# Relative values of an attention layer: table stationary in column strips, probabilities streaming, and new places for the pieces of work

## The chip, the cores and the metric

The kernel is one program on one core of a Trainium2 chip. The metric is the device time of one launch in microseconds (us), median of several executions. All data are fp32. The engines are PE (TensorE: weight loads and matmuls), DVE (VectorE), ACT (ScalarE), POOL (GpSimd), and SP (SyncE), which here only issues transfers.

## The reference, cut to what matters

A batch of 8 sequences of 256 tokens with 128 features passes two layers, each an attention and a feed-forward part with a residual. The change touches only the first attention: 16 heads of 8 features, with learned relative keys and relative values, clipped at a distance of 20.

```python
pos = jnp.arange(S)                                   # S = 256
idx = jnp.clip(pos[None, :] - pos[:, None], -MAX_REL, MAX_REL) + MAX_REL   # MAX_REL = 20
rk2 = rel_k[idx]; rv2 = rel_v[idx]
attn1 = jnp.einsum('bhqd,bhkd->bhqk', q, k)
attn2 = jnp.einsum('bhqd,qkd->bhqk', q, rk2)          # relative scores
attn = jax.nn.softmax((attn1 + attn2) / scale, axis=-1)
w1 = jnp.einsum('bhqk,bhkd->bhqd', attn, v)
w2 = jnp.einsum('bhqk,qkd->bhqd', attn, rv2)          # relative values
x = (w1 + w2).transpose(0, 2, 1, 3).reshape(B, S, E)
out = x @ Wo.T + bo
```

After it come (all unchanged): an attention over the heads of one token with a gated mixture of 8 matrices ("feed"), a Taylor attention ("second"), and a mixture of experts with routing ("late").

## The kernel before

One sequence is called a batch t here, from 0 to 7. Its work is cut into pieces: `norm0` to `blocks` (layer norm, projections, tables of queries), `scores`, `turn`, `relative`, `keep_rv`, `weigh`, `back`, `divide`, `project_out` (first attention), `norm1` to `experts` (feed), `norm3` to `turn4` (second), `route` to `store` (late). Every engine has its own list of pieces of all batches. The list is made from a table of numbers, one for each piece and engine (`ENGINE_AT`, with corrections in `MOVED` for batches 0, 6 and 7): batch t's piece stands at t * 480 plus its number, and the engine works through the pieces in that order and no other. So pieces of three or four batches alternate on each engine. Between engines there are only semaphores.

The first attention of a batch, in the words that the rows use:

- A row group i holds 8 queries of all 16 heads: 128 rows. There are 32 groups, 16 in each half c of the queries. `scores` takes two groups of each half (a quad; 8 quads): L1147 multiplies block-diagonal queries `qbd` with the keys `kT` (256 columns), L1157 adds the relative scores from `qr` and a table `tkw`. Both work in four 64x64 quarters of PE's array at once. DVE takes row maxima (`nmx`, L832), ACT the exponentials (`pm`, L547).
- `turn` transposes `pm` (L1168); ACT moves the result to `pT` (L555).
- `relative` (L1186, and L1189 for the groups near the border of the halves): for each group i the 128x128 probabilities `pT` are the stationary operand and a stretch of the table `tv` is the moving one. Its 64 useful columns are 8 possible distances x 8 features; each of the 128 rows needs the 8 of its own query, and the rest is computed for nothing. The number of columns is 128 for 24 of the 32 groups and 64 for 8. There are 16 such pieces in a batch, one after about each `turn`. ACT copies the sums to `rvs` four times a batch (`keep_rv`, L531).
- SP then stores, for each of the 8 queries of a group, the wanted 8 columns to DRAM (L457, 8 transfers) and, when all have landed, loads them back as `relo` (L460, L462), rows being queries now (`relative_out`).
- `weigh` (L1210) multiplies the probabilities with the values: `v9` is stationary in four column strips of 32, `pT` streams with 128 columns. `back` (L1221) transposes the sums, and `divide` on DVE adds `relo` (L840) and divides by the sums of the probabilities. Then come `turn_out`, `project_out` and the feed part, whose longest DVE stretch begins with `prod<-q,kv` (L883).

SP's queue, in its order: for batch t first `relative_out(t - 1)`, then the load of `xin` for t + 1, then `rows(t + 1)`: queries to DRAM (L439) and back in another layout, `qc` (L448), from which POOL makes `qr`.

Of the kernel before, what the change touches and what calls it, by code (L numbers as in the profile page):

```python
# [100 lines left out]
FEED_AT = [585, 592, 602, 611, 626, 643, 652, 662, 664, 670, 673, 673, 673, 684, 699, 704, 707, 713, 718, 740, 741, 743,  # L101
           759, 774, 781, 813, 816, 840, 855, 882, 907, 910, 920, 946, 958, 963]
# [3 lines left out]
SECOND_AT = [974, 1031, 1059, 1088, 1112, 1141, 1156, 1173, 1175, 1177, 1192, 1220, 1221, 1227, 1236, 1257, 1268, 1274,  # L106
             1303, 1358]
LATE = once("route", "rank") + counted("chunk", NCH + 2) + once("turn_rw") + counted("join", 1 + NP) + once("store")
LATE_AT = [1360, 1366, 1378, 1392, 1408, 1427, 1436, 1442, 1475, 1527, 1555, 1579, 1597, 1630, 1638, 1657, 1659, 1660,
           1675, 1701, 1733, 1760, 1800, 1812]  # L110
LISTS = ("PREPARE", "ATTENTION", "FEED", "SECOND", "LATE")
ALL = PREPARE + ATTENTION + FEED + SECOND + LATE
ALL_AT = PREPARE_AT + ATTENTION_AT + FEED_AT + SECOND_AT + LATE_AT
ENGINE_AT = {"PE": [-445.5, -339, -278, -249.5, -90, 113, 163, 0, 60, 120, 177.5, 241, 302.5, 360, 420, 38.5, 77, 96, 144.5,
# [15 lines left out]
             "DVE": [-354.5, -314, -290.5, -188, -88, 87, 141, 0, 60, 120, 178.5, 240, 301.5, 357.5, 420, 43, 65, 90, 131.5, 143,  # L130
# [1360 lines left out]
```

## Time and profile before

| what | value |
|---|---|
| time, median of 3 runs | 733.3 us (732.82 to 733.8) |
| span of the profiled execution, first to last instruction | 736.6 us |
| PE busy, matmuls | 646.7 us (88%) |
| DVE busy | 548.8 us (75%) |
| ACT busy | 381.3 us (52%) |
| POOL busy | 146.1 us (20%) |
| mean granted TensorE clock, share of full | 0.958 |

The page does not give the profiled execution's own device time beside its span; the span alone is 3.3 us (0.45%) above the median. The busy time of an engine is the union of its instructions' times, and a matmul's end is modelled, so that neighbours on PE overlap a little. What a row of matmuls costs PE is therefore read better from the start of one row to the start of the next than from its duration. An fp32 matmul stands in the trace as two records with a weight load each.

### The profile page before, as it was taken

To read this page: it belongs to the slowest core of one execution; us is meant where nothing else is said; L and a number is where in the kernel's file an instruction comes from. 1 tells how busy PE (TensorE), PEld (TensorE's weight loads), DVE (VectorE), ACT (ScalarE), POOL (GpSimd) and SP (SyncE) were. 2 spreads that over 40 slices of the span, in tenths; PEclk is the share of its full clock that TensorE was granted. 3 is DMA by queue.
4 is the path that set the end of the run, shared out by engine and by line. 5 is a ranking of instruction groups with operands and counts; after the bars stand their busy time and mean duration, and the time that the engine had idled before them with its cause. 6 is when DMAs were issued, how large, how long until landed. Compare 5 with 4: busy or idle time off the path is not lost.

```text
span 736.6 us, 16761 instructions
## 1 busy us (share of the span) xinstructions
PE 646.7 (88%) x6432; PEld 517.3 (70%) x6432; DVE 548.8 (75%) x1337; ACT 381.3 (52%) x907; POOL 146.1 (20%) x178
## 2 busy tenths in 40 slices
PE   2698577987999999999999999899999998789987
PEld 1576355765787688778876788678876886467666
DVE  2432596679868986899689976898779966977375
ACT  3375245456655654674566565575466454413532
POOL 2413201330233023300521051302330012010100
PEclk9799589999999999999999999999999999887999
DMA  5502000200110002000210011000200010000000
GB/s 132 227 2 24 14 1 9 23 9 1 15 16 10 1 16 22 11 1 1 27 21 1 1 24 16 9 1 9 30 2 1 2 15 9 1 8 0 2 8 7
DMA packets 75908, 13.43 MB, mean 18 GB/s; under 512 B 69803, under 2 KB 74933, under 8 KB 75701
## 3 DMA queue, kind: packets, MB, share of 16 engines
q1 hardware_dynamic: 73202, 10.78, 8.1%
q8 instruction: 51, 0.84, 0.5%
q0 software_dynamic: 384, 1.05, 0.5%
q10 hardware_dynamic: 2244, 0.55, 0.3%
q14 instruction: 27, 0.22, 0.1%
HBM read 8.95 MB, written 3.16 MB: 16 GB/s over the span
## 4 chain that ended last, share of the span: by engine, by line
PE 41%; DVE 28%; issue 18%; ACT 6%; POOL 3%; DMA 2%; SPq 1%; POOLq 0%; ACTq 0%; DVEq 0%
PE bank L1147 5%; DVE prod L883 5%; DVE lg L889 4%; PE bank L1168 4%; PE bank L1354 4%; PE bank L1270 4%; PE bank L1355 3%; DVE prod L908 3%; PE bank L1210 3%; DVE at L914 3%; DVE nmx L832 3%; ACT pm L547 3%; PE bank L1186 3%; PE bank L1157 2%; DVE xo L1062 1%
## 5 line engine op out<-in xcount | busy, mean ns | idle before, releaser
L547 ACT ACTIVATE pm<-bank,nmx 128x256 f32<-128x256 f32 x256 | 100.3, 480 | 58.7 <-DVE nmx L832 58.5
L832 DVE TENSOR_REDUCE nmx<-bank 128x2 f32<-128x512 f32 x128 | 82.1, 683 | 44.5 <-PE bank L1157 44.4
L555 ACT ACTIVATE pT<-bank 128x512 f32<-128x512 f32 x128 | 76.5, 598 | 65.0 <-PE bank L1168 64.0
L1147 PE MATMUL bank<-kT,qbd 64*64 64x256 f32 x1024 | 87.7, 405 | 10.4 <-POOL qr L657 9.3
L1168 PE MATMUL bank<-w,pm 128*128 128x128 f32 x512 | 81.9, 284 | 16.2 <-ACT pT L555 10.0
L612 ACT ACTIVATE ha<-bank,w 128x256 f32<-128x256 f32 x104 | 49.6, 477 | 67.5 <-PE bank L1355 67.5
L1168 PEld LDWEIGHTS bank<-w,pm 128*128 128x128 f32 x512 | 59.8, 145 | 29.8 <-ACT pm L547 15.9
L1186 PE MATMUL bank<-tv,pT 128*128 128x128 f32 (+1 forms) x512 | 79.7, 278 | 0.2 <-ACT pT L555 0.2
L1042 DVE SCALAR_TENSOR_TENSOR hu<-bank,w,ha 128x256 f32<-128x256 f32 x104 | 49.9, 480 | 36.5 <-ACT ha L612 35.7
L1186 PEld LDWEIGHTS bank<-tv,pT 128*128 128x128 f32 x512 | 70.0, 195 | 6.0 <-issue 4.4
L1354 PE MATMUL bank<-xfT,w 128*128 128x256 f32 x208 | 67.7, 408 | 3.7 <-DVE hu L1042 3.5
L1355 PE MATMUL bank<-xfT,w 128*128 128x256 f32 x208 | 63.3, 387 | 0.0
L706 POOL TENSOR_TENSOR rs_c<-ve_c,expo 128x2 f32<-128x2 f32 x8 | 5.6, 699 | 273.8 <-DVE ve_c L788 273.8
L1157 PE MATMUL bank<-tkw,qr 64*64 64x96 f32 (+1 forms) x1024 | 55.5, 265 | 0.0
L1157 PEld LDWEIGHTS bank<-tkw,qr 64*64 64x64 f32 x1024 | 46.5, 139 | 12.2 <-issue 1.2
L961 DVE SCALAR_TENSOR_TENSOR x<-bank,gl,x 128x128 f32<-128x128 f32 x128 | 35.9, 344 | 23.3 <-PE bank L1270 23.2
L597 ACT ACTIVATE sq<-bank,half_root 128x512 f32<-128x512 f32 x64 | 40.4, 684 | 18.8 <-PE bank L1309 18.6
L1147 PEld LDWEIGHTS bank<-kT,qbd 64*64 64x64 f32 x1024 | 32.3, 138 | 24.9 <-issue 20.8
L1381 PE MATMUL bank<-w,hu 128*128 128x256 f32 x128 | 41.3, 405 | 4.5 <-DVE xo L1062 3.6
L1355 PEld LDWEIGHTS bank<-xfT,w 128*128 128x128 f32 x208 | 40.5, 195 | 5.6
L657 POOL TENSOR_TENSOR qr<-qc,half_mask 128x512 f32<-128x512 f32 x31 | 33.4, 1097 | 54.1 <-DMA qc<-d_qdh 54.1
L1354 PEld LDWEIGHTS bank<-xfT,w 128*128 128x128 f32 x208 | 33.7, 194 | 14.4 <-DVE hu L1042 9.7
(203 smaller groups left out, 1294.1 us busy)
## 6 DMA issues: line engine op xcount, KB each, us to landing
w<-wpack_dram SPq DMA_DIRECT2D x1, 3944.0 KB, 11.9
xin<-x_in_dram SPq DMA_DIRECT2D x8, 128.0 KB, 2.1
d_qdh<-qdh SPq DMA_DIRECT2D x8, 128.0 KB, 1.8
d_rv<-rvs SPq DMA_DIRECT2D x64, 16.0 KB, 2.2
out_dram<-xo POOLq DMA_DIRECT2D x8, 128.0 KB, 2.3
qc<-d_qdh SPq DMA_DIRECT2D x15, 64.0 KB, 3.7
tv<-d_ev SPq DMA_DIRECT2D x1, 736.0 KB, 4.5
w<-wpack_dram SPq DMA_DIRECT2D x1, 513.0 KB, 5.2
```

Source lines behind the costliest of these rows:

```text
L547: a = act.activation(pm[:, s % 2, c, j], b_s[c][:, j * S:(j + 1) * S], exp, bias=nmx[:, i:i + 1])
L555: act.activation(view(pT, (c * RTC + 2 * s) * C * P, [[1, 2 * C * P]]), b_t[:], copy).then_inc(pT_ready[0], 1)
L612: act.activation(ha[:, n % 2], late_bank(t, "chunk", n)[:, 0:S], idn, scale=0.5, bias=wc("b1", IN_TURN[n], IN_TURN[n] + 1)).then_inc(a_rea ...
L832: v.tensor_reduce(nmx[:, i:i + 2], b_s[c][:].rearrange("p (j k) -> p j k", j=2), AX_X, ALU.max, negate=True).then_inc(max_ready[0], 1)
L1042: v.scalar_tensor_tensor(hu[:, n], late_bank(t, "chunk", n)[:, S:2 * S], wc("b3", IN_TURN[n], IN_TURN[n] + 1), ha[:, n % 2], ALU.add, ALU. ...
L1147: mm(b_s[c][cols:cols + P // 2, j * S:(j + 1) * S], qbd[rows:rows + P // 2, i], kT[rows:rows + P // 2, t % 2, u], start=True, stop=False, ...
L1157: a = mm(b_s[c][cols:cols + P // 2, j * S + lo:j * S + hi], qr[rows:rows + P // 2, i], tkw[rows:rows + P // 2, KB // QI - 1 - i % (KB // Q ...
L1168: a = nc.tensor.transpose(b_t[:, (j * 2 + kc) * P:(j * 2 + kc + 1) * P], chunk(pm[:, s % 2, c, j], kc), ident)
L1186: a = mm(b_rv[:, at:at + n], pT[:, i, c], tv[:, v0 * D0:v0 * D0 + n], start=True, stop=not corner)
L1354: mm(bk[:, 0:S], wc("W1", q * P, q * P + P), xfT[:], start=True, stop=True)
L1355: mm(bk[:, S:2 * S], wc("W3", q * P, q * P + P), xfT[:], start=True, stop=True).then_inc(ab_ps[0], 1)
L1381: mm(o, chunk(hu[:, 3 * n + 2], c), wc("W2rem", e * E, (e + 2) * E), start=True, stop=False, skip_group_check=True)
```

## The change

`relative` becomes two pieces in a batch instead of 16, each for half of the row groups of both halves c. The operands change places: four table rows (four distances x 8 features, 32 columns) are the stationary operand in one of PE's four column strips, and the probabilities of four queries of all heads (64 columns) stream. A piece has 32 such matmuls and 5 more near the borders (74 in a batch against 38 before). ACT copies the sums twice in a batch instead of four times and sorts them on the way (a read with a step of four elements). SP stores four times for each copy, once for each quarter that a query needs, and loads four times; the first half of this goes between the load of `xin` and `rows(t + 1)`, the second after `rows(t + 1)`. `relo` now has features in the outer place, and `divide` reads it with a step. Half of `Wo`'s rows change places for one of the two halves (`wo_turned`, loaded once), and `weigh` counts its heads in another order. The relative scores take only the columns in which the table is not zero: 27 to 83 (46, 46, 46, 51, 59, 67, 75, 83 within each 64 queries, less where the sequence ends) instead of 96 or 128. All numbers of places are new, with corrections for every batch on every engine.

```diff
+QG = P // D0 // 4            # 4 queries
+RG = P // QG
-            def relative_values(t, x):
-                s, c = divmod(x, C)
-                pe.wait_ge(*raised(pT_ready, t, x + 1))
-                ...
-                for j in range(2):
-                    i = c * RTC + 2 * s + j
-                    at = (c * 4 + i % 4) * QI * D0
-                    n = QI * D0 * (2 if i % 4 < 3 else 1)
-                    v0 = S - QI - i % RTC * QI - TV0
-                    corner = RTC - CORNER <= i < RTC + CORNER
-                    a = mm(b_rv[:, at:at + n], pT[:, i, c], tv[:, v0 * D0:v0 * D0 + n], start=True, stop=not corner)
-                    if corner:
-                        ...
+            def relative_values(t, n):
+                pe.wait_ge(*raised(pT_ready, t, HALVES // 2 * (n + 1)))
+                pe.wait_ge(*raised(rv_kept, t, n))
+                ...
+                for T in range(4 * n, 4 * n + 4):
+                    for c in range(C):
+                        for j in range(4):
+                            g = 4 * T + j
+                            out_ = b_rv[j * MT:(j + 1) * MT, (c * 4 + T % 4) * QG * H0:(c * 4 + T % 4 + 1) * QG * H0]
+                            cols = lambda kc: view(pT, ((c * RTC + g // 2) * C + kc) * P + g % 2 * QG, [[QI, H0], [1, QG]])
+                            window = lambda table, x: table[:, x * D0:x * D0 + MT]
+                            a = mm(out_, window(tv, S - QG - QG * g - TV0), cols(c), start=T % 4 == 0 and c == 0, stop=True,
+                                   skip_group_check=True, tile_position=(0, j * MT))
+                            ends = g >= (P - REL) // QG if c == 0 else g < REL // QG
+                            if ends:
+                                ...
+                                a = mm(out_, window((tv_right, tv_left)[c], x), cols(1 - c), start=False, stop=True,
+                                       skip_group_check=True, tile_position=(0, j * MT))
+                a.then_inc(rv_ps[0], 1)
@@ scores, relative part
-                        at = u * KB - NEAR
-                        lo, hi = max(0, at), min(S, at + WIN)
+                        at, first = u * KB - NEAR, i * QI
+                        lo, hi = max(0, min(u * KB, first - REL + 1)), min(S, first + QI + REL - 1)
@@ keep_rv on ACT
-                    act.activation(view(rvs, n * S, [[RTC * QI * D0, C], [1, S]]), b_rv[:], copy).then_inc(rv_kept[0], 1)
+                    act.activation(view(rvs, n * 512, [[QG * H0, 512 // (QG * H0)], [H0, QG], [1, H0]]),
+                                   view(b_rv, 0, [[QG * H0, 512 // (QG * H0)], [1, QG], [QG, H0]]), copy).then_inc(rv_kept[0], 1)
@@ SP
+            def relative_out(t, n):
+                sp.wait_ge(*raised(rv_kept, t, n + 1))
+                ...
+                for q in range(QG):
+                    ...
+                    sp.dma_start(dst, src).then_inc(rv_out[0], 16)
+                sp.wait_ge(*raised(rv_out, t, 16 * QG * (n + 1)))
+                row = C * E
+                for q in range(QG):
+                    dst = bass.AP(relo[:].tensor, (n * P // 2 + q) * row, [[QG * row, RG // 2], [E, C], [1, E]])
+                    sp.dma_start(dst, d_rv[q, n].rearrange("c g d h -> g c (d h)")).then_inc(relo_in[0], 16)
             for t in range(B):
-                if t:
-                    relative_out(t - 1)
                 if t < B - 1:
                     ...  # xin for t + 1
+                relative_out(t, 0)
+                if t < B - 1:
                     rows(t + 1)
-            relative_out(B - 1)
+                relative_out(t, 1)
@@ divide on DVE
-                                    view(relo, n * E, [[D0, H0], [1, D0]]), ALU.add).then_inc(o_steps[0], 1)
+                                    view(relo, n * E, [[1, H0], [H0, D0]]), ALU.add).then_inc(o_steps[0], 1)
@@ tables at the start, DVE: tv comes in as rows and is copied once with a step
+                v.tensor_copy(view(tv, 0, [[MT, TV // QG], [QG, D0], [1, QG]]),
+                              view(hu, 0, [[MT, TV // QG], [1, D0], [D0, QG]])).then_inc(tables_ready[0], 1)
```

PE's order where a batch in the middle of the program goes from its last row groups to `weigh` (L1210 before): before, the last relative matmuls stand in three places between transpositions, expert matmuls (L1354, L1355) and the feed's products (L1270).

```order
L1168 MATMUL bank<-w,pm 128x128 x4
L1186 MATMUL bank<-tv,pT 128x128
L1189 MATMUL bank<-tv_right,pT 128x128
L1186 MATMUL bank<-tv,pT 128x64
L1189 MATMUL bank<-tv_right,pT 128x64
L1270 MATMUL bank<-w,hT 128x256 x2
L1186 MATMUL bank<-tv,pT 128x128
L1186 MATMUL bank<-tv,pT 128x64
L1354 MATMUL bank<-xfT,w 128x256
L1355 MATMUL bank<-xfT,w 128x256
L1210 MATMUL bank<-pT,v 32x128 x32
```

In the changed kernel (line numbers are its own: L1401 is `weigh`, L1375 and L1380 `relative`, L1461 the feed's products, L1545 and L1546 the expert matmuls) the same place reads:

```order
L1401 MATMUL bank<-pT,v 32x128 x32
L1461 MATMUL bank<-w,hT 128x256 x2
L1545 MATMUL bank<-xfT,w 128x256
L1546 MATMUL bank<-xfT,w 128x256
L1358 MATMUL bank<-w,pm 128x128 x4
L1461 MATMUL bank<-w,hT 128x256 x2
L1545 MATMUL bank<-xfT,w 128x256
L1546 MATMUL bank<-xfT,w 128x256
L1375 MATMUL bank<-pT,tv 32x64 x20
L1380 MATMUL bank<-pT,tv_right 32x64
L1375 MATMUL bank<-pT,tv 32x64 x5
L1380 MATMUL bank<-pT,tv_right 32x64
```

The first `weigh` now stands ahead of the last `turn` and of the second `relative` block, which is one lump of 37 matmuls.

SP's queue before, one batch of it with what each transfer waits for:

```order
L439 DMA d_qdh<-qdh 128x2x128 [waits qc_in,qdh_ready]
L448 DMA qc<-d_qdh 64x32x8 [waits qr_ready,qdh_out]
L448 DMA qc<-d_qdh 64x32x8
L457 DMA d_rv<-rvs 16x32x8 [waits on_ready,rv_kept]
L457 DMA d_rv<-rvs 16x32x8 x7
L460 DMA relo<-d_rv 128x128 [waits rv_out]
L462 DMA relo<-d_rv 128x64 x2
L473 DMA xin<-x_in_dram 128x2x128 [waits xres_ready,xn_ready]
```

And in the changed kernel (L639 stores, L644 loads of `relo`, L620 and L629 `rows`, L656 `xin`):

```order
L656 DMA xin<-x_in_dram 128x2x128 [waits xres_ready,xn_ready]
L639 DMA d_rv<-rvs 32x8x16 [waits on_ready,rv_kept]
L639 DMA d_rv<-rvs 32x8x16 x3
L644 DMA relo<-d_rv 16x2x128 [waits rv_out]
L644 DMA relo<-d_rv 16x2x128 x3
L620 DMA d_qdh<-qdh 128x2x128 [waits qc_in,qdh_ready]
L629 DMA qc<-d_qdh 64x32x8 [waits qr_ready,qdh_out]
L629 DMA qc<-d_qdh 64x32x8
L639 DMA d_rv<-rvs 32x8x16 [waits rv_kept]
L639 DMA d_rv<-rvs 32x8x16 x3
L644 DMA relo<-d_rv 16x2x128 [waits rv_out]
L644 DMA relo<-d_rv 16x2x128 x3
```

The first half of the stores and loads now stands ahead of the next batch's `rows`, the second half behind it.

## Rows read from the trace of the kernel before

**Rows 1.** The page, part 1: busy us (share of the span) and instructions.
```profile
PE 646.7 (88%) x6432; PEld 517.3 (70%) x6432; DVE 548.8 (75%) x1337; ACT 381.3 (52%) x907; POOL 146.1 (20%) x178
```

**Rows 2.** Windows: stretch, length, busy us (instructions) by engine, clock, DMA share, GB/s.
```profile
20.80:62.40 41.60, 35.33 (x410) 28.41 (x410) 13.81 (x27) 25.41 (x61) 9.98 (x12) 0.90 0.28 97
62.40:135.30 72.90, 52.46 (x589) 41.84 (x591) 45.23 (x88) 31.03 (x76) 15.66 (x18) 0.81 0.08 10
135.30:205.20 69.90, 60.45 (x707) 47.59 (x710) 55.84 (x133) 39.81 (x96) 17.50 (x22) 1.00 0.09 11
...
285.20:365.20 80.00, 76.94 (x809) 62.52 (x812) 67.10 (x164) 46.62 (x113) 18.53 (x22) 1.00 0.08 11
...
524.60:603.00 78.40, 74.44 (x791) 60.74 (x790) 65.35 (x154) 44.46 (x104) 10.56 (x14) 1.00 0.04 7
603.00:736.60 133.60, 112.47 (x717) 85.38 (x716) 92.63 (x258) 47.36 (x106) 12.28 (x15) 0.92 0.03 6
```

**Rows 3.** Chain of waits in order of time: start us, us, what.
```profile
94.15 2.36 DVE prod L883 x2
...
159.41 2.36 DVE prod L883 x2
...
626.46 2.36 DVE prod L883 x2
```

**Rows 4.** PE's timeline, relative matmuls of batch 4: start us, us, what.
```profile
318.25 0.83 PE L1186 MATMUL bank<-tv,pT 128*128 128x128 f32 x6
318.93 0.39 PE L1189 MATMUL bank<-tv_left,pT 128*128 128x128 f32 x2
319.15 0.33 PE L1186 MATMUL bank<-tv,pT 128*128 128x64 f32 x2
319.32 0.39 PE L1078 MATMUL bank<-w,xn 128*128 128x128 f32 x2
```

**Rows 5.** PE's timeline: a `weigh` piece and a quad of scores.
```profile
285.17 1.95 PE L1210 MATMUL bank<-pT,v 128*32 128x128 f32 x64
287.06 1.13 PE L1270 MATMUL bank<-w,hT 128*128 128x256 f32 x4
...
288.98 0.66 PE L1147 MATMUL bank<-kT,qbd 64*64 64x256 f32 x8
289.46 0.40 PE L1157 MATMUL bank<-tkw,qr 64*64 64x96 f32 x8
289.63 0.67 PE L1147 MATMUL bank<-kT,qbd 64*64 64x256 f32 x8
...
290.44 0.70 PE L1354 MATMUL bank<-xfT,w 128*128 128x256 f32 x2
```

**Rows 6.** PE's timeline: two matmuls with eight columns.
```profile
352.91 0.51 PE L1348 MATMUL bank<-w,xfT 128*128 128x8 f32 x4
353.27 0.64 PE L1186 MATMUL bank<-tv,pT 128*128 128x128 f32 x4
```

**Rows 7.** SP's timeline, stores and loads of relative values, batch 3, then batch 0.
```profile
284.98 6.08 SPq L457 DMA_DIRECT2D d_rv<-rvs  x8
...
292.98 0.91 SPq L462 DMA_DIRECT2D relo<-d_rv  x2
```

**Rows 8.** DVE's timeline, the addition that uses them in `divide`.
```profile
75.21 0.29 DVE L840 TENSOR_TENSOR on<-bank,relo 128x128 f32<-128x128 f32 x1 [3.95 <-DMA relo<-d_rv]
...
296.49 0.23 DVE L840 TENSOR_TENSOR on<-bank,relo 128x128 f32<-128x128 f32 x1
```

**Rows 9.** Waits: who for whom, us in total, times, longest.
```profile
PE bank L1221 <- DVE on L840: 5.2, 3, 4.4
```

**Rows 10.** Groups by line on ACT: busy us, mean ns | idle before, releaser.
```profile
L531 ACT ACTIVATE rvs<-bank 128x512 f32<-128x512 f32 x32 | 19.2, 600 | 7.1 <-PE bank L1186 7.1
```

**Rows 11.** The page, part 6: transfers, KB each, median us to landing.
```profile
d_rv<-rvs SPq DMA_DIRECT2D x64, 16.0 KB, 2.2
relo<-d_rv SPq DMA_DIRECT2D x16, 32.0 KB, 2.0
```

More of the change, by code:

```diff
@@ L146 @@
-MOVED = {0: [-488, -493, -365, -195, -212, -252, -189, 0, 0, 0, 0, 0, 0, 0, 0, 9, -11, 5, 12, 10, 10.5, 10, 6, -1, 7, 5,
[18 rows of a table removed]
-PIECES = sorted([(at, k, piece) for k, (piece, at) in enumerate(zip(ALL, ALL_AT))])
-def in_turn(at):
-    placed = [(t * PERIOD + at[k] + (MOVED[t][k] if t in MOVED else 0), k, t) for k in range(len(ALL)) for t in range(B)]
+ENGINE_AT = {
[8 rows of a table added]
+    "ACT": [-392.5, -327, -654, -451, -75.5, 57, 229, 0, 60, 157.9, 164, 245, 301.5, 360, 420, 46.3, 59.8, 106, 164.1, 165, 199.7, 217,
[6 rows of a table added]
+    "DVE": [-354.5, -807, -290.5, -188, -300, 87, 141, 0, 92.8, 120, 178.5, 240, 346.8, 357.5, 420, 43, 65, 90, 131.5, 143, 166, 203,
[6 rows of a table added]
+    "POOL": [-321.6, -292, -217.5, -205, -147.5, -27, 38, 0, 60, 120, 178.5, 245, 301.5, 360, 420, 12, 64, 91, 168.5, 181, 193, 215,
[6 rows of a table added]
@@ new lines, with in_turn @@
+MOVED = {
[61 rows of a table added]
+    "ACT": {0: {0: -488, 1: -493, 4: -212, 5: -252, 6: -189, 7: 46.2, 10: 35.8, 16: -11.3, 18: -6.3, 19: 10, 22: 6, 23: 14.5, 28: 15, 29:
[56 rows of a table added]
+    "DVE": {0: {0: -488, 2: -365, 3: -195, 5: -252, 6: -189, 9: 23.1, 15: 9, 16: -11, 17: 5, 18: 12, 19: 10, 20: 10.5, 21: 10, 22: 6, 23:
[54 rows of a table added]
+    "POOL": {0: {0: -481.9, 1: -493, 2: -365, 3: -195, 4: -212, 5: -252, 6: -98.9, 15: 9, 16: -11, 17: 5, 18: 12, 19: 10, 20: 10.5, 21: 10,
[33 rows of a table added]
+def in_turn(engine):
+    at, moved = ENGINE_AT[engine], MOVED[engine]
+    placed = [(t * PERIOD + at[k] + moved.get(t, {}).get(k, 0), k, t) for k in range(len(ALL)) for t in range(B)]
@@ L170, in in_turn @@
     return [(t, ALL[k]) for _, k, t in sorted(placed)]
-TURNS = {engine: in_turn(at) for engine, at in ENGINE_AT.items()}
-assert len(ALL_AT) == len(ALL)
+TURNS = {engine: in_turn(engine) for engine in ENGINE_AT}
+assert all(len(at) == len(ALL) for at in ENGINE_AT.values())
 W_COLS = [("ident", P), ("head_mask", H0), ("query_mask", QI), ("head_mask3", H1), ("earlier", NE * NE), ("half", P),
@@ L267, in build @@
         pT = sb("pT", P, RT, C, P)
-        rvs = sb("rvs", P, RT, QI * D0)
-        relo = sb("relo", P, C, E)
+        rvs = sb("rvs", P, 2, 512)
+        relo = sb("relo", P, C, D0, H0)
+        wo_turned = sb("wo_turned", P, E)
         oT = sb("oT", P, C, 512)
@@ L325, in build @@
         ek, ev = sq[:].rearrange("p h c q -> p (h c q)")[:, 0:EK], hu[:].rearrange("p n s -> p (n s)")[:, 0:EV * D0]
+        tv_rows = hu[:].rearrange("p n s -> p (n s)")[:, 0:TV * D0]
         ht = sb("ht", P, 2, S)
@@ L448, in rows @@
                     sp.dma_start(*own_rows(half)).then_inc(qc_in[0], 16)
[L450 to L462 removed]
+            def relative_out(t, n):
+                sp.wait_ge(*raised(rv_kept, t, n + 1))
+                if n == 0:
+                    sp.wait_ge(*raised(on_ready, t, 0))
+                for q in range(QG):
+                    src = bass.AP(rvs[:].tensor, (QG - 1 - q) * 2 * 512 + n * 512 + q * H0, [[QG * 2 * 512, P // QG], [QG * H0, 512 // (QG * H0)], [1, H0]])
+                    dst = bass.AP(d_rv.tensor, (q * 2 + n) * C * E * RG // 2, [[H0, P // QG], [H0 * P // QG, 512 // (QG * H0)], [1, H0]])
+                    sp.dma_start(dst, src).then_inc(rv_out[0], 16)
[4 more added lines that the diff above has]
+                    sp.dma_start(dst, d_rv[q, n].rearrange("c g d h -> g c (d h)")).then_inc(relo_in[0], 16)
             rows(0)
@@ L466, in _ @@
             sp.dma_start(w[:, n0:], wpack[:, n0:]).then_inc(w_in1[0], 16)
+            for half in range(2):
+                to = (1 - half) * P // 2
+                sp.dma_start(wo_turned[to:to + P // 2], wc("WoT", p0=half * P // 2, p1=(half + 1) * P // 2)).then_inc(turned_in[0], 16)
             for t in range(B):
-                if t:
-                    relative_out(t - 1)
                 if t < B - 1:
@@ L1121, in piece @@
                     pe.wait_ge(*raised(onT_ready, t, 1))
+                    if t == 0:
+                        pe.wait_ge(turned_in[0], 32)
                     for c in range(C):
-                        a = mm(chunk(b_o, c), chunk(onT, c), wc("WoT"), start=True, stop=True)
+                        a = mm(chunk(b_o, c), chunk(onT, c), wo_turned[:] if c else wc("WoT"), start=True, stop=True)
                     a.then_inc(wo_ps[0], 1)
@@ L1206, in weigh @@
                             h = i * PER + j
-                            v0 = (kc + C * (kc != c)) * V9 + h * (D0 + 1)
-                            row = (h + c * D0) % H0 * QI
+                            v0 = (kc + C * (kc != c)) * V9 + (h + c * D0) % H0 * (D0 + 1)
+                            row = h * QI
                             a = mm(b_o[j * MT:(j + 1) * MT, i * P:(i + 1) * P], v9[:, v0:v0 + MT],
```

60 lines of the change are left out of this document (14 added, 46 removed), and 276 rows, old and new, of tables (ENGINE_AT, MOVED).

## The prediction

> **What bounds the kernel now.** I read the page's busy times first, then windows cut at the start of each batch's `weigh`, then PE's timeline inside one window. PE leads with 646.7 of 736.6 us, DVE follows with 548.8 [rows 1]. The windows show where that holds. From 205.2 to 603.0 us five batches pass at (603.0 - 205.2) / 5 = 79.6 us each, and in the one that stands there PE is busy 76.9 of 80.0 us, DVE 67.1, ACT 46.6, at the full clock [rows 2]. So PE's own work sets the period, with some 3 us of waits; DVE would allow 13 us less. The head is another matter. Batch 0's attention takes 41.6 us with PE busy for 35.3, and the next 72.9 us hold 52.5 us of PE work at a granted share of 0.81, part of it at the lower level of 1.2 GHz [rows 2]: there PE waits for DVE's feed stretch, which begins at 94.15 us for batch 0 and at 159.41 for batch 1 [rows 3]. From the feed stretch of batch 7 at 626.46 to the end are 110 us that hold no first attention any more [rows 3].
>
> **Relative values, before.** Starts give the price: from 318.25 to 319.32 us there are ten records, five matmuls, so 0.214 us each [rows 4]. A batch has 38: 8.1 us.
>
> **Relative values, after.** The old trace has no 64-column stream in strips; the nearest row is `weigh`, the same array form and the same operand streaming with 128 columns: 32 matmuls from 285.17 to 287.06, 0.236 us for each four that run side by side [rows 5]. That is about what one full-array matmul of 128 columns costs (0.214), so the four share the time and the columns set it. That loading can set it instead is seen at eight columns: 0.18 us a matmul for 128 weight columns [rows 6]; 32 columns would need a quarter, 0.045 (estimate). With 64 columns a four should cost 0.118; if nothing came from the shorter stream, 0.236. A block has 37 matmuls, 9.25 fours: 1.1 to 2.2 us. Two extras. Ten border matmuls a batch follow another in the same strip; if each waits for its predecessor they add at most 10 x 0.107 (half the 128-column price) = 1.1 us. And changing the form of the array costs something: in a quad the first pair of groups takes 0.65 us (288.98 to 289.63), the second, which ends in a change to the full array, 0.81 [rows 5]; two blocks have four such changes, up to 0.64 us. Ends for a batch: 2.2 and 6.1 us. I take 3.5, near the lower end because `weigh` shows columns, not loads, as the price. Saved: 4.6 us a batch.
>
> **Relative scores.** Four matmuls of 256 columns and four of 96 and 128 take the 0.65 us above, so columns set that too: 384 columns, 1.7 ns each. The widest of a four falls from 128 to 46, 46, 46, 51, 59, 67, 75 and 83, 59 on average: 0.117 us less for each of 16 fours, 1.9 us a batch; nothing if the next weights can't come sooner. I take 1.6, because loading 64 columns (half of 0.18 us) would still hide. The Trainium skill, TensorEngine Tiling (Array Packing), section "Instruction Overhead", says that a matmul of one column lasts as long as one of about 60. By that rule five of the eight widths count as 60, the mean is 66, and the saving 1.7 us instead of 1.9; no run here shows it yet.
>
> **What this does to the period.** PE's work falls by 6.2 us (2.0 to 7.9). What is late next is the answer of the stores. Before, the first store goes out at 284.98, the last load at 292.98 to 293.89, and DVE adds at 296.49: 11.5 us [rows 7, 8]. Now half of it has gone earlier; the rest is a copy (0.6) [rows 10], four stores at 6.08 / 8 = 0.76, four loads at 0.91 / 2 = 0.46, and two landings, 2.2 and 2.0 [rows 7, 11]: 9.7 us. In the new order two quads (2.9), `weigh` (1.9), a transposition (0.4) and six pairs of full-array matmuls (about 0.96 each, from 287.06 to 288.98 for two [rows 5]) stand between the second block and the first `back`: 11 us. It just covers; behind `back`, `divide` on DVE and everything behind it in DVE's order would wait, and PE's second `back` with it. Such waits were 5.2 us in all before [rows 9]. I charge 0.8 us a batch for this and for DVE being 90% full. Period: 79.6 - 5.4 = 74.2 us, bounds -1.2 to -7.9 (the gain of 2.0 less the 0.8, and 7.9 with no new wait). Five periods: -27 us (-6 to -40).
>
> ACT loses two copies a batch, 1.2 us, behind PE. Its reads now step by four elements; were they twice as slow, the two would cost what the four did. That sits in the chain to `divide` alone, 0.6 us. The one more copy of `tv` at the start and the load of `wo_turned` lie beside DMA and PE work of the head, long before their users; if not, 2 us once. In SP's queue `rows(t + 1)` now waits for the first half's stores, some 3.0 + 2.2 us and a copy; `relative 0` stands far ahead of the last row groups, and a batch's `rows` had some 15 us before its scores, so I charge nothing.
>
> **Head and tail.** Batch 0's attention loses 8.1 us of PE work that stood between its quads and gets 3.5 back in two lumps: -4. Its `divide` had waited 3.95 us for `relo` on DVE, and PE 4.4 us with it [rows 8, 9]: -4. Then batch 1's scores now fill PE while DVE does batch 0's feed stretch, so batch 1's attention is over when that stretch ends, and PE spends less of these 72.9 us at the low clock: of the 65.3 us between the two feed stretches [rows 3] I take 5 off. Together -13 (-4 to -20). The interval to batch 2 is bound less by PE (60.5 of 69.9 us): -2. The tail has the same work in nearly the same order: 0 (3 either way).
>
> Sum against the profiled span: 736.6 - 27 - 13 - 2 = 694.6 us. The median lies 3.3 us under that span, so 691.5, say **692 us**.
>
> **Rivals.** (a) Less: waits take the place of the matmuls. In favour: DVE goes from 84 to 90% full and the cover of the store chain is about 1 us. Against: PE waits only 3 us a period now. With -2 a period, -8 in the head and -1: 736.6 - 19 - 3.3 = 714. (b) More: the new places also take out half of PE's present waits, and the head gives its full 20: -7.9 x 5 - 20 - 3 is 62, 671; a middle case 677. DVE's 67 us a period leave room for it. (c) The strips don't run side by side at 64 columns: 74 x 0.107 + 0.64 = 8.6 us, nothing saved, and only the scores' 1.6 a batch stay, less the waits: about -1 a period and -7 in the head, 721. Against it stands `weigh`, whose strips do. (d) Slower: the two blocks are bound by how fast PE can begin instructions. A batch has 148 records there instead of 76; from (8.1 - 0.64) / 148 = 50 ns a record the relative values save nothing, and from 61 ns the scores' 1.6 us are gone too. At 70 ns a period is 1.3 us longer, and the lump ahead of `weigh` costs the head as much: 733.3 + 6 x 1.3 is 741. Against it: `weigh` has 64 records in 1.89 us, 30 ns each, while it streams [rows 5]. A rule of the Trainium skill lies in this direction: TensorE: Matmul & The Clock Gate, section "Wait — 56ns, not 53.3ns?", gives about 62 ns a matmul where the sequencer's program decodes it and 25 ns as the floor otherwise. By the first figure relative values would cost 9.8 us a batch and the kernel would be slower as in (d); the 30 ns of `weigh` say that it doesn't hold in this run.
>
> **How the numbers follow.** The forecast, in a band of some 9 us either way, 0.56; (a) 0.20; (b) 0.13; (c) 0.05; (d) 0.04; a change of nothing 0.02. The range from 674 to 717 holds the forecast, nearly all of (a) and most of (b), and leaves out (c), (d) and the far ends. The likeliest case alone is 683 to 702. What a measurement can tell from no change is about 0.2%, 1.5 us. Faster 0.94, the same 0.02, slower 0.04.
>
> **What would show it.** In the profile after: the starts of `weigh` in the middle 73.5 to 75.5 us apart; 32 + 5 matmuls of a relative block in 1.3 to 2.2 us from its start to the next row's; a quad in 1.2 to 1.3 us instead of 1.46; DVE 88 to 92% busy in a period and PE near 95%, at the full clock; batch 1's feed stretch at 142 to 152 us. Wrong would be: a block over 3 us, records in it more than 50 ns apart, the clock under 0.95 in the middle, or DVE's wait for `relo` in every batch.

## The result, and the profile after

The changed kernel takes 729.7 us (median of 20 runs, 723.5 to 736.3), beside 736.0 us for the kernel before (20 runs on the same chips). The ratio is 0.9916, with a 95% interval of 0.9889 to 0.9943: 0.8% faster, some 6 us, where 41 were predicted and the range ended at 717. The profiled execution has a span of 729.2 us (before 736.6).

The page of the changed kernel, part 1, answers to [rows 1]:

```profile
PE 605.6 (83%) x7008; PEld 462.2 (63%) x7008; DVE 565.3 (78%) x1338; ACT 374.3 (51%) x891; POOL 148.5 (20%) x178
```

PE has lost 41.1 us of busy time; 8 x 6.2, some 50, were forecast. DVE, from which nothing was taken, is 16.5 us busier. Both lines matter below. The windows of the changed kernel, cut at the starts of `weigh` as in [rows 2]:

```profile
21.00:70.20 49.20, 33.14 (x510) 23.84 (x514) 16.12 (x30) 24.39 (x58) 16.07 (x16) 0.78 0.26 85
70.20:121.50 51.30, 36.90 (x550) 26.66 (x538) 38.44 (x70) 27.38 (x65) 6.78 (x8) 0.83 0.09 14
121.50:192.80 71.30, 56.57 (x769) 40.77 (x768) 57.78 (x125) 37.25 (x93) 14.98 (x18) 0.91 0.05 8
274.90:350.30 75.40, 69.28 (x873) 54.19 (x872) 68.06 (x156) 45.95 (x111) 18.29 (x21) 1.00 0.06 10
510.70:593.30 82.60, 75.45 (x961) 58.16 (x960) 71.26 (x177) 47.72 (x112) 15.48 (x18) 1.00 0.06 8
593.30:729.20 135.90, 109.85 (x709) 83.94 (x708) 93.62 (x254) 45.86 (x104) 13.14 (x16) 0.92 0.02 6
```

Read by this mark, the five middle periods last (593.3 - 192.8) / 5 = 80.1 us, against 79.6 before, and the whole gain seems to lie in the head. The mark misleads: in the new order `weigh` of a batch stands elsewhere against the feed stretch of the batch before. DVE's feed stretch keeps its place in the batch, so its first instruction is the better mark. DVE's timeline of the changed kernel at these four places, for batches 0, 1, 2 and 7 [rows 3]:

```profile
99.04 2.36 DVE L1071 TENSOR_TENSOR prod<-q,kv 128x1024 f32<-128x1024 f32 x2
...
158.70 2.36 DVE L1071 TENSOR_TENSOR prod<-q,kv 128x1024 f32<-128x1024 f32 x2
...
230.08 1.22 DVE L1071 TENSOR_TENSOR prod<-q,kv 128x1024 f32<-128x1024 f32 x1
...
618.12 1.23 DVE L1071 TENSOR_TENSOR prod<-q,kv 128x1024 f32<-128x1024 f32 x1
```

Before, these stood at 94.15, 159.41, 233.19 and 626.46. So batch 0 is 4.9 us later, batch 1 is 0.7 earlier, the interval from 1 to 2 gives 2.4 more, the five intervals from 2 to 7 give 5.2, and the tail takes 0.9 back: -0.7 - 2.4 - 5.2 + 0.9 = -7.4, the difference of the two spans. From here on "the five intervals" means this stretch between the feed of batch 2 and that of batch 7. Its window (length, PE busy, PEld, DVE, ACT, POOL, granted clock, DMA share, GB/s), in the kernel before:

```profile
233.19:626.46 393.27, 375.16 (x3890) 304.53 (x3882) 329.25 (x798) 225.40 (x540) 78.20 (x92) 1.00 0.07 10
```

and in the changed kernel:

```profile
230.08:618.12 388.04, 350.96 (x4227) 272.49 (x4226) 339.23 (x797) 220.57 (x528) 79.57 (x92) 0.98 0.07 11
```

PE's busy time falls by 24.2 us, but its idle time (length less busy) rises from 18.1 to 37.1 us. That is the riddle of this case in two lines: PE's work was taken away, and PE waits instead. For what, the waits of the changed kernel in this stretch tell (who for whom, us in total, times, longest):

```profile
PE bank L1266 <- DVE hh L1121: 5.6, 3, 3.2
PE bank L1475 <- ACT k L773: 3.8, 5, 0.8
PE bank L1266 <- DVE hh L980: 3.2, 2, 2.7
PE bank L1412 <- DVE on L1028: 3.1, 4, 1.3
PE bank L1432 <- DVE q L1060: 3.1, 3, 1.7
```

Many waits of 0.8 to 3.2 us, on DVE and ACT, of many kinds and few of each. The longest is the first. PE's, DVE's and POOL's timeline of the changed kernel around it:

```profile
423.05 3.27 DVE L1121 TENSOR_SCALAR hh<-xl,rs_b 128x128 f32<-128x128 f32 x2
423.45 0.73 POOL L878 TENSOR_TENSOR x<-x,xl 128x256 f32<-128x256 f32 x1
424.14 2.08 POOL L837 TENSOR_TENSOR qbd<-qT,half_mask 128x512 f32<-128x512 f32 x2
...
426.37 0.47 PE L1266 MATMUL bank<-w,hh 128*128 128x128 f32 x1 [3.22 <-DVE hh L1121]
```

`scale2`, two DVE instructions that take 0.28 us each elsewhere, lasts 3.27 us here. The second of the two alone takes 2.82, the longest of its kind, and ends at 426.32, just behind POOL's sum `x2` and two `qbd` products (423.45 to 426.22). PE stands for 3.22 us, and then runs at a lower clock. Three windows of the changed kernel, before the gap, behind it and later:

```profile
418.00:423.00 5.00, 4.93 (x60) 3.90 (x58) 4.89 (x18) 3.74 (x12) 1.70 (x3) 1.00 0.11 17
426.30:432.90 6.60, 6.53 (x79) 5.83 (x80) 5.20 (x20) 1.89 (x5) 3.76 (x4) 0.59 0.29 19
434.00:440.00 6.00, 5.98 (x97) 4.88 (x96) 3.63 (x12) 2.62 (x5) 1.34 (x2) 1.00 0.01 3
```

The mean granted clock is 0.59 for 6.6 us, most of it at the lower level of 1.2 GHz, between two stretches at the full 2.4. The prediction had priced neither.

The parts that it did price are there. PE's timeline of the changed kernel, `weigh`, a block of relative values (43 of its 74 records stand in the row shown), and a quad [rows 4, 5]:

```profile
274.91 1.95 PE L1401 MATMUL bank<-pT,v 128*32 128x128 f32 x64
...
280.07 0.81 PE L1375 MATMUL bank<-pT,tv 128*32 128x64 f32 x43
...
281.32 0.70 PE L1545 MATMUL bank<-xfT,w 128*128 128x256 f32 x2
...
298.36 0.66 PE L1337 MATMUL bank<-kT,qbd 64*64 64x256 f32 x8
298.85 0.29 PE L1347 MATMUL bank<-tkw,qr 64*64 64x59 f32 x8
...
299.62 0.70 PE L1471 MATMUL bank<-h3T,w 128*128 128x256 f32 x2
```

A block takes 281.32 - 280.07 = 1.25 us, a quad 299.62 - 298.36 = 1.26.

### The profile page after: what moved, and what is told of

Its sections match the earlier page's. It is cut to its first block, busy times and chain, and to the rows that moved or that the text cites. A ratio compares the mean times of both kernels' runs of the same rounds, so it can differ in the third digit from the quotient of the medians.

```text
span 729.2 us, 17909 instructions
## 1 busy us (share of the span) xinstructions
PE 605.6 (83%) x7008; PEld 462.2 (63%) x7008; DVE 565.3 (78%) x1338; ACT 374.3 (51%) x891; POOL 148.5 (20%) x178
## 4 chain that ended last, share of the span: by engine, by line
issue 36%; PE 29%; DVE 16%; DMA 6%; POOL 6%; ACT 4%; SPq 3%; POOLq 0%; ACTq 0%; DVEq 0%
PE bank L1545 3%; PE bank L1337 3%; PE bank L1461 3%; PE bank L1546 3%; PE bank L1358 3%; DVE nmx L1020 2%; PE bank L1500 2%; DVE at L1102 2%; DVE xo L1250 2%; DVE hh L1121 1%; DVE prod L1096 1%; PE bank L1401 1%; PE bank L1266 1%; DMA xin<-x_in_dram 1%; DMA d_rv<-rvs 1%
## 5 line engine op out<-in xcount | busy, mean ns | idle before, releaser
L733 ACT ACTIVATE pm<-bank,nmx 128x256 f32<-128x256 f32 x256 | 100.4, 483 | 34.5 <-DVE nmx L1020 34.1
L1358 PE MATMUL bank<-w,pm 128*128 128x128 f32 x512 | 86.7, 295 | 20.7 <-ACT pT L741 12.4
L1337 PE MATMUL bank<-kT,qbd 64*64 64x256 f32 x1024 | 85.5, 425 | 15.3 <-POOL qr L843 11.0
L1358 PEld LDWEIGHTS bank<-w,pm 128*128 128x128 f32 x512 | 61.7, 150 | 38.3 <-issue 19.1
L1545 PE MATMUL bank<-xfT,w 128*128 128x256 f32 x208 | 69.3, 416 | 5.1 <-DVE hu L1230 5.1
L1546 PE MATMUL bank<-xfT,w 128*128 128x256 f32 x208 | 64.2, 391 | 0.0
L1347 PEld LDWEIGHTS bank<-tkw,qr 64*64 64x64 f32 x1024 | 42.2, 145 | 19.7 <-issue 5.1
L1337 PEld LDWEIGHTS bank<-kT,qbd 64*64 64x64 f32 x1024 | 28.9, 143 | 31.0 <-issue 20.2
L1546 PEld LDWEIGHTS bank<-xfT,w 128*128 128x128 f32 x208 | 41.2, 198 | 6.1
L1545 PEld LDWEIGHTS bank<-xfT,w 128*128 128x128 f32 x208 | 33.8, 197 | 14.9 <-DVE hu L1230 10.3
L1500 PE MATMUL bank<-q3h,k 64*128 64x256 f32 x256 | 36.5, 402 | 7.8 <-ACT sq L783 5.7
L1572 PE MATMUL bank<-w,hu 128*128 128x256 f32 x128 | 39.5, 391 | 2.8 <-DVE xo L1250 1.4
L1574 PEld LDWEIGHTS bank<-w,hu 128*128 128x128 f32 x256 | 38.5, 190 | 3.4
L837 POOL TENSOR_TENSOR qbd<-qT,half_mask 128x512 f32<-128x512 f32 x32 | 34.0, 1084 | 29.7 <-issue 20.0
## 6 DMA issues: line engine op xcount, KB each, us to landing
hu<-d_ev SPq DMA_DIRECT2D x1, 736.0 KB, 4.6
```

What stands on the lines that cost most here:

```text
L733: a = act.activation(pm[:, s % 2, c, j], b_s[c][:, j * S:(j + 1) * S], exp, bias=nmx[:, i:i + 1])
L1337: mm(b_s[c][cols:cols + P // 2, j * S:(j + 1) * S], qbd[rows:rows + P // 2, i], kT[rows:rows + P // 2, t % 2, u], start=True, stop=False, ...
L1347: a = mm(b_s[c][cols:cols + P // 2, j * S + lo:j * S + hi], qr[rows:rows + P // 2, i], tkw[rows:rows + P // 2, KB // QI - 1 - i % (KB // Q ...
L1358: a = nc.tensor.transpose(b_t[:, (j * 2 + kc) * P:(j * 2 + kc + 1) * P], chunk(pm[:, s % 2, c, j], kc), ident)
L1500: a = mm(taylor_bank(t, 2 * n + half)[:, kc * S:(kc + 1) * S], chunk(k3[rows:rows + P // 2], kc), q3h[rows:rows + P // 2, n], start=True, ...
L1545: mm(bk[:, 0:S], wc("W1", q * P, q * P + P), xfT[:], start=True, stop=True)
```

## The experiments

Times are medians; each ratio is to runs of the kernel before on the same chip, with its 95% interval. Theory C: in the new order POOL and DVE collide, and the feed stretch, with all that waits for it, is late. Theory D: DVE's own work in that stretch sets the period. Theory O: the new places cost what the arithmetic gave. Two more, W and P, were formed from the first results; the other letters (N, S, P', F, G) are told where they come up.

**One wait more on POOL.**

```
  elif name == "turn2":
      pool.wait_ge(*raised(y_ready, t, 1))
      pool.wait_ge(*raised(x3_ready, t - 1, 0))
+     pool.wait_ge(*raised(h2_ready, t, 1))
```

> The changed kernel with one wait more: POOL begins the sum x2 (and the qbd products queued behind it) only when DVE has finished scale2 (hh<-xl), so that the two no longer run at once. Theory C (collisions of POOL and DVE in the new order stretch the feed stretch's critical operations): hh<-xl falls from a mean of 905 ns to 350-460, the gap ahead of turn2 on PE goes, and the time falls by 6 to 14 us from 729.7, to 716-724. Theory D (DVE's feed stretch, with its own work, sets the period): DVE loses some 9 us in all by it, of which a part shows, 724-729. Theory O (the new places are at fault): no change within 3 us.

Measured: 718.2 us, ratio 0.9740 (0.9699 to 0.9782), 1.8% better than the changed kernel's 0.9916, by a wait. The group of `scale2` in the changed kernel, and then in this one, whose lines stand one further down (busy us, mean ns | idle before):

```profile
L1121 DVE TENSOR_SCALAR hh<-xl,rs_b 128x128 f32<-128x128 f32 x16 | 13.9, 905 | 1.9 <-POOL rs_b L874 1.7
```

```profile
L1122 DVE TENSOR_SCALAR hh<-xl,rs_b 128x128 f32<-128x128 f32 x16 | 5.5, 393 | 1.9 <-POOL rs_b L874 1.7
```

The five intervals of this kernel:

```profile
227.16:605.83 378.67, 345.35 (x4227) 267.67 (x4226) 333.88 (x797) 220.44 (x528) 79.80 (x92) 1.00 0.07 11
```

The same 4227 PE instructions take 5.6 us less, with the clock at 1.00 in place of 0.98, and PE's idle time falls from 37.1 to 33.3. In the whole launch PE waits 2.7 us for `scale2` instead of 9.2. Theory C holds, and its price lies inside what it expected: a collision of two engines and a PE gap behind it. How much of the clock's part belongs to it, the next section asks.

**The same wait in the kernel before.**

> The kernel before with the same one wait (POOL's sum x2 and the blocks behind it begin after scale2). A control: if the collision is one of the new order, it brings little here, where hh<-xl has a mean of 462 ns against 905: -1 to -4 us, ratio to before 0.995 to 0.999. If the wait is simply good for any order of this kernel, -8 to -12 us, ratio 0.984 to 0.989, and the change itself would then be worth as little as it seemed.

Measured: 742.0 us, 1.0053 (1.0018 to 1.0087). Not even the small gain: `scale2` falls from 462 to 279 ns here as well, and the kernel is 0.5% slower, which no theory had. POOL's sum `x2` now stands 17.2 us in all for `scale2`, against 3.7 in the changed kernel with the wait; that this is the 0.5% isn't shown. So the wait is no general good, and the gain above belongs to the order that the change brought.

**A second wait, for `xn`.** On top of the first:

```
  elif name == "qkv3":
      ...
      pool.wait_ge(*raised(o3_back, t, 0))
+     if t + 3 < B:
+         pool.wait_ge(*raised(xn_ready, t + 3, 1))
```

> The kernel with the wait for scale2, and a second one: POOL begins the q3h products only when DVE has finished xn of the batch three further on. In the profile of the first wait alone, xn is stretched by 6.4 us in 9 of 16 instances, each while POOL runs q3h or the sum xl. Theory C: xn falls to 350-450 ns, 3 to 5 us of DVE time go, and as turn0 and the projections of the next batch wait for it, 1 to 5 us of the time: 713-717. Theory N (xn is early enough that nobody waits): 718, the same within 2 us, or 1 to 3 us slower if q3h is late for the second attention.

Measured: 712.9 us, 0.9658 (0.9609 to 0.9707). `xn` falls from a mean of 736 ns to 340. The five intervals:

```profile
223.61:599.77 376.16, 344.86 (x4227) 268.19 (x4226) 331.55 (x797) 220.50 (x529) 83.81 (x94) 1.00 0.07 11
```

The time lies where theory C had it; theory N, by which nobody waits for `xn`, had 718. With both waits the kernel is 3.4% faster than the kernel before, and PE's busy time in the five intervals is 30.3 us under that of before, close to the prediction's 5 x 6.2 = 31, at the full clock.

**POOL's products in halves.** Each `qbd` and `qr` instruction of the kernel with both waits becomes two:

```
- g.tensor_tensor(view(qbd, i * P // 2, [[P // 2, QI], ...
+ for m in range(0, QI, QI // 2):
+     a = g.tensor_tensor(view(qbd, (i + m) * P // 2, [[P // 2, QI // 2], ...
```

> The kernel with both waits, and POOL's products qbd and qr cut into two instructions of half the size each. With the waits, hb, bi, sc and hh still last 0.9 to 1.1 us instead of 0.17 to 0.34 where one of these products (1.07 us) runs. Theory C (a colliding DVE instruction has to wait until the POOL instruction under way is over): those instances come down to 0.55 to 0.65 us, and the time falls by 1 to 4 us from 712.9, to 709-712. Theory S (POOL takes a share of DVE's rate as long as it is busy): the instances last as long as before, and the time stays or rises by 1 to 2 us, since two halves cost POOL more than one whole.

Measured: 711.2 us, 0.9622 (0.9575 to 0.9670). The intervals overlap, so a gain in time isn't shown. The mechanism is. Here are POOL's and DVE's timelines of the kernel with whole products, and then with halves, where `hb` meets them:

```profile
284.07 2.55 POOL L843 TENSOR_TENSOR qr<-qc,half_mask 128x512 f32<-128x512 f32 x2
...
284.59 2.12 DVE L983 TENSOR_SCALAR hb<-x,mv_c,rs_c 128x128 f32<-128x128 f32 x2
```

```profile
283.97 1.66 POOL L838 TENSOR_TENSOR qbd<-qT,half_mask 128x256 f32<-128x256 f32 x2
285.59 2.02 POOL L846 TENSOR_TENSOR qr<-qc,half_mask 128x256 f32<-128x256 f32 x3
...
285.06 1.23 DVE L987 TENSOR_SCALAR hb<-x,mv_c,rs_c 128x128 f32<-128x128 f32 x2
```

Two `hb` instructions last 2.12 us beside whole products and 1.23 beside halves; alone they take 0.34 each. Here DVE's instruction waits until the POOL instruction under way is over; theory S, by which POOL takes a share of DVE's rate, would have left them as long. The Trainium skill, SBUF — State Buffer, section "Who interferes with whom", says this of DVE's modes that use two ports, which `tensor_scalar` can enter: whichever engine issues first has the shared pair for the whole instruction, and the other is blocked. The traces agree, by 2.12 against 1.23 us. The prediction had not weighed it. One POOL instruction is the usual price but not the most: the `scale2` instruction of 2.82 us above was held across three that followed one another. What decides that, no run shows.

**The new arithmetic at the old places.** The old tables for all engines; the two blocks at the places of relative pieces 7 and 15:

```
+ KEPT = list(range(31)) + [38, 46, 48, 50] + list(range(51, ...))
+ placed = [(t * PERIOD + at[o] + ..., k, t) for k, o in enumerate(KEPT) ...]
```

> The changed arithmetic (strips, trimmed scores, stores that pick) at the places of the kernel before; the two blocks stand where the eighth and the sixteenth relative piece stood, all engines' tables are the old ones. Theory O (the new places are at fault): the saved 5 to 6 us of PE work a batch now show in the period, 74-76 us, and the time is 692-708. Theory D (DVE's feed stretch sets the period whatever PE saves): the middle period stays at 79-80 us, and the head's gain, which came from the order, is lost: 728-740. Theory C: between the two, 715-728, since the collisions go back to those of before.

Measured: 747.8 us, 1.0156 (1.0119 to 1.0193): 1.6% slower than before. Its five intervals:

```profile
235.66:634.16 398.50, 350.31 (x4254) 268.11 (x4246) 333.65 (x798) 220.59 (x530) 78.15 (x92) 0.99 0.07 10
```

PE is busy for 24.9 us less than before and idle for 48.2 instead of 18.1. Theory O falls, and more than that: the places are what made the change a gain, 1.0156 - 0.9916 = 2.4%, 18 us. And the saved PE work by itself made nothing faster. The waits, in the same stretch of this kernel:

```profile
PE bank L1315 <- ACT sq L598: 7.3, 5, 1.8
PE bank L1081 <- DVE hh L795: 6.0, 5, 1.5
PE bank L1173 <- ACT pT L556: 5.1, 9, 1.7
PE bank L1387 <- DVE xo L1065: 4.8, 5, 2.5
```

In the kernel before the same pieces stood for 1.5 us (`sq`), 3.3 (`hh`), 1.3 (`pT`) and 2.5 (`xo`) in its five intervals. PE reaches each of its waiting pieces earlier, and the answer of ACT or DVE isn't there.

**The old arithmetic at the new places**, eight pieces in each lump, ACT's copies moved up so that they can follow:

```
+ PLACE = list(range(31)) + [31] * 8 + [32] * 8 + [33] * 2 + [34] * 2 + ...
```

> The arithmetic of before (16 relative pieces with the values streaming, four copies, wide scores) at the new places: eight pieces at the place of each block, on ACT the copies moved up so that they can follow. Theory O: the new order costs the middle what the arithmetic gave, so this kernel is slower than before by 15 to 30 us, 750-765. Theory D: PE's work of 76.9 us a period is under what the order gives it anyway, the head gains as it did: 728-740. A price of its own: the stores leave only behind the second block, so divide may wait for relo by 2 to 4 us a batch, up to 25 us in all.

Measured: 823.1 us, 1.1187 (1.1140 to 1.1235), far outside all that was expected. PE alone waits 12.5 us for the copies that a lump of eight pieces needs in its midst, and DVE waits up to 7.0 us at a time for ACT's `ha` (4.3 before). It shows that the new places fit the new arithmetic only; for what the order is worth by itself it is no clean measure.

**DVE's work cut, in the changed kernel and in the one with both waits.**

```
- view(q1, ..., [[D0, H0 // 2], [0, H0], [1, D0]]),
+ view(q1, ..., [[D0, H0 // 2], [0, H0], [1, D0 // 2]]),
```

> The changed kernel with DVE's dot products of the feed stretch over 8 of the 16 dimensions of a head (the other half is left out): 8 operations of 1.2 us become 0.6 to 0.65, so DVE's stretch is 4.5 to 5 us shorter a batch, with PE's work as it is. Theory D: nearly all of it shows where that stretch bounds, 3.5 to 5 us in each of seven intervals, 25 to 35 us: 695-705. Theory O: the time stays within 6 us, since PE's order and not DVE's work is what binds: 724-730. Theory C: a small part, 720-730.

> The kernel with both waits, and DVE's dot products over 8 of 16 dimensions (the other half is left out), some 4.5 us less DVE work a batch. Theory D (with the collisions gone DVE's own work binds): 15 to 30 us less, 683-698. Theory W: 3 to 9 us less, as before the waits (729.7 to 722.4), 704-710.

A head has 8 features here, so the edit leaves out 4 of 8, not 8 of 16; `kv` and the sum behind the products are cut in the same way. Measured: 722.4 us, 0.9782 (0.9730 to 0.9835), and 714.4 us, 0.9680 (0.9634 to 0.9726). DVE is busy for 565.3 - 530.8 = 34.5 us less in the first; about 10 us of it show, in theory C's range and not in D's 25 to 35. With both waits 32 us less of DVE work show nothing at all (0.9658 without the cut). Theory D falls: DVE's work is not what binds.

**PE's work put back.** Scores at the old widths, in the changed kernel and in the one with both waits, and the blocks of the changed kernel computed twice over:

```
- lo, hi = max(0, min(u * KB, first - REL + 1)), min(S, first + QI + REL - 1)
+ lo, hi = max(0, at), min(S, at + WIN)
```

```
- for T in range(4 * n, 4 * n + 4):
+ for T in [T for twice in range(2) for T in range(4 * n, 4 * n + 4)]:
```

> The changed kernel with the trimming of the relative scores undone: the old widths of 96 and 128 columns. PE gets back 7.5 to 8 us of work in five periods, 1.5 a batch, spread over the quads. Theory P (a microsecond of PE work has its full price): 12 us more, 741-743. Theory W (an order of pieces that wait for other engines sets the period, so that saved PE work turns into PE's idle time, which rose from 16.2 us to 35.9 in five periods): 1 to 5 us more, 730-735, and PE's idle time in the middle falls by 5 us or more.

> The kernel with both waits, and the trimming of the scores undone. In the changed kernel as it was, the trimming was worth nothing (731.2 against 729.7). Theory P' (the collisions hid what PE saved; without them PE's work has its price again): 8 to 12 us more, 721-725. Theory W (the order of waiting pieces binds still, PE idles 30 us in five periods): 0 to 4 us more, 713-717.

> The changed kernel with each block of relative values computed twice over (the second pass writes the same result): 2.6 to 2.8 us more PE work a batch, in the two lumps. Theory P: 8 x 2.7 = 21 us more, 749-753. Theory W: the lumps stand between pieces that wait, part of it is covered by waits that follow: 6 to 14 us more, 736-744.

Measured: 731.2 us, 0.9914 (0.9878 to 0.9951); 719.1 us, 0.9746 (0.9703 to 0.9788); 745.5 us, 1.0082 (1.0042 to 1.0122). With 12 us of PE work for the wide scores (8 x 1.5), the trimming is worth nothing in the changed kernel (0.9914 against 0.9916) and 0.9746 - 0.9658 = 0.9%, 6.5 us, with both waits. Some 20 us for the second pass of the blocks (16 x 1.25) cost 1.7%, 12 us. So a microsecond of PE work costs 0 to 0.6 us, and the intervals leave 0.2 to 0.4 either way: theory W, an order of pieces that wait for one another, against theory P, the full price. After the waits its price looks higher, though not whole: 719.1 lies between what W and P' had, and the step from 0 to 0.9% is at the edge of what the intervals tell apart.

**The first block in four pieces**, behind the third, fifth and seventh transposition and at the old place, in the kernel with both waits:

```
+ turns[turns.index((t, ("relative", 0)))] = (t, ("relative", 3))
+ for T in range(3):
+     turns.insert(turns.index((t, ("turn", 2 * T + 2))) + 1, (t, ("relative", T)))
```

> The kernel with both waits, and the first block of a batch cut into four pieces of 8 to 10 matmuls, of which three stand behind the third, fifth and seventh transposition, where PE waits for ACT's copy of pT, and the fourth where the block stood. Theory F (the old 16 pieces had filled such waits, and a lump can't): PE's idle time in five periods falls by 2 to 5 us, the time by 1 to 5, 708-712. Theory G (waits go elsewhere, and three more changes of the array's form a batch cost some 0.1 to 0.2 us each): 0 to 4 us more, 713-717.

Measured: 725.5 us, 0.9850 (0.9796 to 0.9903), 2% slower than the one block. Its five intervals:

```profile
236.81:623.72 386.91, 352.96 (x4203) 272.46 (x4202) 333.06 (x798) 220.80 (x529) 83.89 (x94) 0.98 0.07 11
```

PE is busy for 8.1 us more and idle for 33.9 us instead of 31.3, at a clock of 0.98. This profiled execution took 733.7 us, 8 above the median, so its figures may overstate the cost. Theory F falls for these places, and G is too small: why three cuts a batch cost 13 us in all is not settled.

## Why the prediction was wrong

What it said of the operations was right, or too careful. Relative values cost 2 x 1.25 = 2.5 us a batch (taken: 3.5, lower end 2.2), so the strips do run side by side at 64 columns, and (c) and (d) are out. A quad takes 1.26 us (said: 1.2 to 1.3; 1.46 before). DVE waits for `relo` 2.0 us in all, four times, where batch 0 alone had taken 3.95 [rows 8]. Tail: +0.9, said 0 within 3. One slip of the sum, 694.6 less 3.3 being 691.3 and not 691.5, changes nothing.

The step that failed is "What this does to the period". It took PE's own work to set the period, because PE was busy for 76.9 of 80.0 us, and charged 0.8 us a batch for new waits; so it got 74.2. Measured between feed stretches, the period went from 78.7 to 77.6, with PE busy for 90% of it and DVE for 87% (said: near 95, and 88 to 92). In the five intervals the terms were, from one profiled execution of each kernel:

| term | predicted | changed kernel | with both waits |
|---|---|---|---|
| PE busy | -31 | -24.2 | -30.3 |
| PE idle | +4 | +19.0 | +13.2 |
| sum | -27 | -5.2 | -17.1 |

The busy term of -30.3 fits 31 in part by luck. By its rows a batch saves 8.1 - 2.5 = 5.6 us of relative values and 8 x 0.2 = 1.6 us of scores, 36 us in five; some 6 us of other PE busy time came in, and from where was not followed.

The idle term was mis-sized by 15 us, for two reasons. About half of the gap between -27 and -5.2, 11.9 us, goes with the waits on POOL: 5.8 us of idle time and 6.1 us of busy time. The idle part is theory C's, and it repeats. In the four kernels without a wait (changed, wide scores, halved dot products, doubled blocks) PE waits 8.9 to 9.3 us in all for `scale2`, 3.1 to 3.2 us of it at one time; in the six with the first wait or both, 1.9 to 2.7. The clock's part is less sure. It was 0.98 to 0.99 in the five intervals of those four and 1.00 with one wait and with both, but 0.98 to 0.99 again in the four kernels with both waits and another edit; with POOL's products in halves it was 0.51 from 559.0 to 569.5 us, and PE had no gap over 0.74 us from 552 us on to there. The clock of whole launches does rise (medians of 0.946 to 0.956 without a wait, 0.957 to 0.966 with), so a gain is there and its size is open. Nothing in the prediction looked at what POOL would do beside DVE's `scale2` and `xn` in the new order, though the order of both engines was there to read.

The other 9.9 us are put down to theory W because they are left; no run takes them away. A PE that is busy for 95% of a period isn't bound by its work if many of its pieces wait for an answer of ACT or DVE that the work in between had hidden. The old matmuls were that cover: without them, at the old places, all of the 25 us, and 5 more, turned into idle time. That kernel has the two lumps and the new stores too, so the missing cover is argued from its waits and not isolated. The rival (a) had this mechanism, at 714 and a chance of 0.20, but left a gain of 2 us a period, where 1.0 was left.

The head failed too. Batch 1's feed stretch was to begin at 142 to 152 us, 13 earlier than before; it began at 158.70. The interval from batch 0's feed came as said, 59.7 us (65.3 less 5), but not by less time at the low clock, as was said. Its window before, and then in the changed kernel:

```profile
94.15:159.41 65.26, 52.25 (x612) 42.12 (x608) 47.73 (x101) 31.82 (x79) 16.31 (x19) 0.92 0.09 11
```

```profile
99.04:158.70 59.66, 43.93 (x608) 32.68 (x608) 49.02 (x97) 25.88 (x67) 16.54 (x19) 0.86 0.09 13
```

The clock fell from 0.92 to 0.86; what shrank is PE's busy time, by 8.3 us. That the number fits is in part luck. But batch 0's attention, which should give 8 us, takes 4.9 more. PE's waits from 21.0 to 70.2 us in the changed kernel:

```profile
PE bank L1337 <- POOL qr L843: 11.0, 2, 9.4
PE bank L1358 <- ACT pm L733: 6.7, 5, 1.9
PE bank L1266 <- DVE xn L980: 5.0, 1, 5.0
```

The 9.4 us at the start stood before too (9.3). But the exponentials `pm` had cost 3.4 and 0.9 us, and `xn` nothing. Between two quads of batch 0 there is nothing else to do, so where the relative matmuls stood PE now waits 1.42 us for ACT's `pm`, three times; `turn0` of batch 1 has moved up to a place where DVE hasn't its `xn` yet; and `qr` is 1.6 us late for batch 1's scores, a cost that the prediction had set to nothing: SP stands for 28.7 us at the first half's stores with `rows` of batch 1 behind them.

What stays open is how much of the remaining idle time, 31.3 us in the five intervals with both waits, another order would recover, what the clock's part is worth, and the 0.5% that the control lost.

## What to carry to other kernels

A busy share of 95% on one engine doesn't price its work: where every engine runs a fixed order, count how many of its pieces wait for another engine, and what work now covers each wait, before crediting a saving. When an order changes, lay POOL's and DVE's instructions side by side as well; a wait that keeps them apart can be worth more than the arithmetic. And choose a mark for the period that keeps its place in the batch when the order moves.

## What the runs showed of the hardware

A DVE instruction and a POOL instruction that collide stand still one behind the other. It goes both ways, and also for products of two tensors: in the kernel with both waits, POOL's last product `q3h`, its sum `xl` and DVE's `prod` of two inputs meet.

```profile
374.27 2.03 POOL L891 TENSOR_TENSOR q3h<-q,half_mask 128x512 f32<-128x512 f32 x2 [1.96 <-DVE xn L983]
376.26 1.70 POOL L870 TENSOR_TENSOR xl<-xl,r 128x256 f32<-128x256 f32 x1
...
375.58 3.46 DVE L1074 TENSOR_TENSOR prod<-q,kv 128x1024 f32<-128x1024 f32 x2
```

The sum, 0.7 us elsewhere, takes 1.70, and two `prod`, 2.36 us elsewhere, take 3.46.

In four strips PE begins instructions faster than the prediction's 30 ns a record: 74 records in 1.25 us, 17 ns each, which is also under the 25 ns that the prediction quotes as a floor. And ACT's copy of `rvs`, which now reads with a step of four elements, takes the same 0.60 us as before [rows 10].

Widths under 60 columns still count in the relative scores. From its start to that of the second, the first pair of groups of a quad takes 0.57 us where the widest matmul of a four has 46 columns (315.92 to 316.49), 0.59 with 59 (298.36 to 298.95) and 0.61 with 75 (303.25 to 303.86). The 13 columns from 46 to 59 cost 0.02 us, what the prediction's 1.7 ns each make, so the rule of about 60 columns that it quotes doesn't show in these rows.
